# A fused four-layer kernel on one core: the newer attention's first and last units are issued in other places, and its loads in other pieces

## What is computed

```python
x = x + _L0_attn_ref(_layernorm(x))          # older attention
x = x + _L0_ffn_ref(_layernorm(x), ...)      # routed low-rank experts
x = x + _L1_attn_ref(_layernorm(x), ...)     # newer attention
x = x + _L1_ffn_ref(_layernorm(x), ...)      # low-rank experts again

# _L1_attn_ref, cut:
q = _rmsnorm(x @ wq_a.T, q_a_ln_w) @ wq_b.T          # 32 heads of 128
q_nope, q_pe = (q[..., :64], q[..., 64:])
ckv, k_pe = (ckv_kpe[..., :64], ckv_kpe[..., 64:])   # ckv_kpe = x @ wkv_a.T
scores = einsum('bqhd,bkhd->bhqk', q_full, k_full) * softmax_scale   # q_pe and k_pe rotated
attn = softmax(where(causal, scores, min))
out = einsum('bhqk,bkhd->bqhd', attn, v).reshape(B, S, H * 128)
return out @ wo.T
```

## Time and profile before

| | us |
|---|---|
| median of 3 runs (lowest, highest) | 1612.07 (1609.93, 1612.68) |
| the profiled execution: its time, its span | 1615.58, 1613.8 |
| PE busy in the span | 1545.7 (96%) |
| DVE, ACT, POOL busy | 1008.0, 878.5, 811.8 |
| mean granted clock of TensorE | 0.993 |

### The profile page before, as it was taken

One profiled execution on the slowest core, in us unless ns is written; L12 is line 12 of the kernel. 1 busy time (PEld: TensorE's weight loads), 2 busy tenths in 40 slices (PEclk: granted clock), 3 DMA queues, 4 the chain that ended last, 5 costly groups with the idle time before them and its releaser, 6 DMA issues. The chain is left out here.

```text
span 1613.8 us, 31992 instructions
## 1 busy us (share of the span) xinstructions
PE 1545.7 (96%) x12384; PEld 951.8 (59%) x12384; DVE 1008.0 (62%) x2745; ACT 878.5 (54%) x1665; POOL 811.8 (50%) x706
## 2 busy tenths in 40 slices
PE   5998999999989999999999999899999999999998
PEld 4656555555556777777767777644444444466564
DVE  8898767776778888888888888732110100344433
ACT  7787323323759999999999999931210000211110
POOL 4223345446938888888888888720110000244450
PEclk9999999999999999999999999999999999999999
DMA  9993244545829999999999999997763331233331
GB/s 365 306 333 142 67 102 136 154 131 140 156 70 160 192 181 176 191 181 189 187 179 182 192 174 173 181 224 217 176 165 77 96 84 21 82 66 79 92 79 65
DMA packets 556103, 248.78 MB, mean 154 GB/s; under 512 B 498096, under 2 KB 530992, under 8 KB 555824
## 3 DMA queue, kind: packets, MB, share of 16 engines
q1 hardware_dynamic: 555952, 246.74, 66.4%
HBM read 73.68 MB, written 48.23 MB: 76 GB/s over the span
## 5 line engine op out<-in xcount | busy, mean ns | idle before, releaser
L2078 POOL TENSOR_TENSOR xb<-xb 128x1280 f16<-128x1280 f32 x128 | 335.8, 2623 | 8.2 <-ACT xb L1981 8.1
L1973 ACT ACTIVATE xb<-bk,D_sv,qw_c 128x512 f32<-128x512 f32 (+3 forms) x512 | 289.3, 623 | 4.7 <-DVE D_sv L2036 4.4
L2027 DVE TENSOR_REDUCE bk<-bk 128x1 f32<-128x512 f32 (+3 forms) x512 | 227.5, 490 | 18.1 <-PE bk L1923 17.3
L1981 ACT ACTIVATE xb<-xb 128x1280 f16<-128x1280 f32 x128 | 162.6, 1271 | 15.4 <-DMA xb<-xb 11.7
L92 POOL TENSOR_SCALAR mv<-mv 128x1 f32<-128x1 f32 x64 | 28.2, 440 | 280.1 <-DVE mv L87 279.0
L1914 PE MATMUL bk<-kTh,D_QTh 128*128 128x512 f16 (+3 forms) x512 | 153.7, 300 | 6.4 <-ACT xb L1973 6.3
L1915 PE MATMUL bk<-kTl,D_QTh 128*128 128x512 f16 (+3 forms) x512 | 153.4, 300 | 0.0
L1916 PE MATMUL bk<-kTh,D_QTl 128*128 128x512 f16 (+3 forms) x512 | 146.8, 300 | 0.0
L1938 PE MATMUL D_t<-vh,xb 128*128 128x65 f16 x1280 | 132.2, 194 | 5.6 <-DVE D_on L2046 3.5
L1939 PE MATMUL D_t<-vl,xb 128*128 128x65 f16 x1280 | 132.3, 193 | 0.0
L1940 PE MATMUL D_t<-vh,xb 128*128 128x65 f16 x1280 | 131.7, 194 | 0.0
(11 more groups left out here) (355 smaller groups left out, 4385.1 us busy)
## 6 DMA issues: line engine op xcount, KB each, us to landing
od<-D_os SPq DMA_DIRECT2D x32, 512.0 KB, 3.8
xd<-xb SPq DMA_DIRECT2D x16, 512.0 KB, 4.4
ow_raw<-mwd SPq DMA_DIRECT2D x16, 512.0 KB, 4.7
xb<-xd SPq DMA_DIRECT2D x16, 512.0 KB, 5.9
out_x<-xb SPq DMA_DIRECT2D x16, 512.0 KB, 2.8
xb<-in_x SPq DMA_DIRECT2D x6, 1024.0 KB, 13.2
A_wo<-in_wo SPq DMA_DIRECT2D x6, 1024.0 KB, 7.2
ow_raw<-in_w SPq DMA_DIRECT2D x16, 384.0 KB, 4.6
```

What stands on the lines that cost most here:

```text
L1973: m = e.activation(p[:, AT[i]:AT[i] + N], Sb[n % 4][:, c:c + N], ACT.Exp, scale=qw.col(qw.NEG, g), bias=s[:, 7 - i:8 - i])
L1981: e.activation(P2[u % 3][:, 0:1280], P[u % 3][:, :], ACT.Copy).then_inc(s_ph, 1)
L2027: m = e.tensor_reduce(minima(u, i), Sb[n % 4][:, c:c + N], AX.X, ALU.min)
L2078: e.tensor_tensor(P2[u % 3][:, 1280:2560], P[u % 3][:, :], P2[u % 3][:, 0:1280], ALU.subtract).then_inc(s_pl, 1)
```

## The change

It changes the order of the work and the size of some transfers; the same numbers are computed.

- **C, queries and scores.** Queries 0 and 1 are issued behind tile 13 and 2 and 3 behind tile 14, on all engines. Unit 0's turn, its split (`act_high`, `dve_low`) and its scores stand in C's tail, in banks bk0 to bk2. Its split halves lie in `keep`. D starts with unit 1's turn and unit 0's masks.
- **C, weights.** The fourth split of output weights (`ow.act_high(3)`, `ow.dve_low(3)`) moves from D's first units into C's tail. Each raw slice is loaded in two transfers of 256 KB; in C they stand one behind each feed transfer of tiles 4 to 9, and group 0's query weights, one transfer at C's start before, are two behind those of tiles 10 and 11.
- **D, output products.** The slices 0 to 3 of tile j = 2 are multiplied in units 124 to 127, between the first and the second part of the scores, into the query banks. Tiles 0 and 1 get slices 0 to 3 in steps 128 to 131 (129 to 132 before), and slice 4 of all three is in step 132 (`AHEAD` = 5); E starts at slice 5.
- **D, turned pieces.** Pieces p = 0, 1 and 2 of j = 0 to 2 are issued in units 42, 48, 54, 74, 80, 86, 106, 112 and 118. Before, p = 0 was in units 123 to 125, p = 1 in steps 130 to 132, and p = 2 in E.

```diff
 class OutWeights:
-    AHEAD = 4
+    AHEAD = 5
-    def sp_load(self, e, w, kt):
+    def sp_load(self, e, w, kt, halves=(0, 1)):
         w.wait_ge(self.s_ml, kt - 2)
-        e.dma_start(self.raw[kt % 3][:, :].rearrange("p (f n) -> p f n", f=2),
-                    self.mwd[:, :, kt, :].rearrange("f p n -> p f n")).then_inc(self.s_m[kt % 3], 16)
+        for f in halves:
+            e.dma_start(self.raw[kt % 3][:, 512 * f:512 * f + 512], self.mwd[f, :, kt, :]).then_inc(self.s_m[kt % 3], 16)
...
 def projections
   def pe(e):
+        def scores(part):
+            w.wait_ge(s_tl, 4)
+            w.wait_ge(s_vl, (14, 15, 13)[part])
+            qu.pe_scores(e, w, 0, part, bk[part], kT)
...
-            if t >= 2:
+            if 2 <= t < NT - 1:
                 turn_qk(t - 2)
-        query(0)
-        query(1)
+            if t == NT - 3:
+                query(0)
+                query(1)
+            if t == NT - 2:
+                query(2)
+                query(3)
+                turn_qk(NT - 3)
+        w.wait_ge(s_vl, 13)
+        qu.pe_turn(e, w, 0, bk[2], ident)
         turn_qk(NT - 2)
-        query(2)
+        scores(0)
         turn_qk(NT - 1)
-        query(3)
+        scores(1)
+        scores(2)
   def act(e):
...
-        squares(NT - 1)
+            if t >= NT - 2:
+                for u in (2 * (t - NT + 2), 2 * (t - NT + 2) + 1):
+                    qu.act_nope(e, w, u)
+        ow.act_high(e, w, 3)
         high_qk(NT - 3)
         high_v(NT - 2)
-        qu.act_nope(e, w, 0)
-        qu.act_nope(e, w, 1)
+        squares(NT - 1)
+        qu.act_high(e, w, 0, bk[2])
         high_qk(NT - 2)
         high_v(NT - 1)
-        qu.act_nope(e, w, 2)
         high_qk(NT - 1)
-        qu.act_nope(e, w, 3)
   def sp(e):
-        e.dma_start(qu.wb[0][:, :, :, :], wbs[0]).then_inc(s_wb, 16)
         for t in range(3, NT):
             feed.sp_turn(e, w, NT + t)
-            if 8 <= t < 11:
-                ow.sp_load(e, w, t - 8)
+            if 4 <= t < 10:
+                ow.sp_load(e, w, t // 2 - 2, (t % 2,))
+            if 10 <= t < 12:
+                e.dma_start(qu.wb[0][:, t - 10, :, :], wbs[0, :, t - 10, :, :]).then_inc(s_wb, 16)
...
 def attention
-    HIGH, LOW = {-2: 3, NU: 4, NU + 1: 5}, {-1: 3, NU + 1: 4, NU + 2: 5}
+    HIGH, LOW = {NU: 4, NU + 1: 5}, {NU + 1: 4, NU + 2: 5}
   def pe(e):
                 w.wait_ge(s_exp, n - 3)
...
+                qu.pe_scores(e, w, u, part, Sb[n % 4], kT)
+                if part == 0 and u >= NU - 4:
+                    w.wait_ge(s_qn, NU)
+                    w.wait_ge(s_qm, NU)
+                    ow.pe_product(e, w, 2, u - NU + 4)
...
-            if NU < u <= NU + ow.AHEAD:
+            if NU <= u < NU + ow.AHEAD:
                 w.wait_ge(s_exp, 3 * NU)
                 w.wait_ge(s_bias, 2 * NU)
-                w.wait_ge(s_qn, NU)
-                w.wait_ge(s_qm, NU)
-                for j in range(ow.G):
-                    ow.pe_product(e, w, j, u - NU - 1)
+                for j in range(2 if u < NU + 4 else ow.G):
+                    ow.pe_product(e, w, j, u - NU)
   def sp(e):
-            if u == NU - 5:
-                w.wait_ge(s_ot[0], 16 * 15)
-            if NU - 5 <= u < NU - 5 + ow.G:
-                ow.sp_turn_piece(e, u - NU + 5, 0)
-            if NU + 2 <= u < NU + 2 + ow.G:
-                ow.sp_turn_piece(e, u - NU - 2, 1)
+            for p in range(3):
+                for j in range(ow.G):
+                    if u == 42 + 32 * p + 6 * j:
+                        w.wait_ge(s_ot[0], 16 * (4 * p + 3))
+                        ow.sp_turn_piece(e, j, p)
...
 def out_projection
   def sp(e):
-        for p in range(2, 4):
-            if p == 3:
-                w.wait_ge(ow.s_o[0], 16 * G)
-            for j in range(G):
-                ow.sp_turn_piece(e, j, p)
-                ow.sp_load(e, w, next(loads))
+        w.wait_ge(ow.s_o[0], 16 * G)
+        for j in range(G):
+            ow.sp_turn_piece(e, j, 3)
+            ow.sp_load(e, w, next(loads))
```

More of the change, by code:

```diff
@@ L523, in __init__, with pe_turn, act_high, dve_low @@
         self.t2b = [keep[:, 2048 + 256 * i:2304 + 256 * i].rearrange("p (h d) -> p h d", h=4) for i in range(2)]
+        self.QT = [[keep[:, 2560 + 256 * i:2816 + 256 * i].bitcast(H16) for i in range(2)]]
         self.s_q, self.s_qn, self.s_qm, self.s_qr = sem("q"), sem("qn"), sem("qm"), sem("qr")
+        self.s_t, self.s_th, self.s_tl = sem("t"), sem("th"), sem("tl")
     def place(self, sb):
         self.qs += [sb(f"qs{i}", [128, 4, 4, 128]) for i in range(1, 3)]
+        self.QT += [[sb(f"QT{x}", [128, 512], H16) for x in "hl"]]
+    def pe_turn(self, e, w, u, ps, ident):
+        g, b, h = self.UNITS[u]
+        q = self.qs[u // 4 % 3]
+        w.wait_ge(self.s_qn, 4 * (u // 4) + 4)
+        w.wait_ge(self.s_qr, 4 * (u // 4) + 4)
+        w.wait_ge(self.s_tl, u)
+        for tt in range(4):
+            i = e.matmul(ps[:, 128 * tt:128 * tt + 128], q[:, tt, h, :], ident, start=True, stop=True, is_transpose=True)
+        i.then_inc(self.s_t, 1)
+    def act_high(self, e, w, u, ps):
+        w.wait_ge(self.s_t, u + 1)
+        e.activation(self.QT[u % 2][0][:, :], ps[:, :], ACT.Copy).then_inc(self.s_th, 1)
+    def dve_low(self, e, w, u, ps):
+        hi, lo = self.QT[u % 2]
+        w.wait_ge(self.s_th, u + 1)
+        e.tensor_tensor(lo[:, :], ps[:, :], hi[:, :], ALU.subtract).then_inc(self.s_tl, 1)
+    TILES = [(3,), (2,), (1, 0)]
+    def pe_scores(self, e, w, u, part, bank, kT):
+        hi, lo = self.QT[u % 2]
+        k0 = 512 * self.UNITS[u][1]
+        w.wait_ge(self.s_tl, u + 1)
+        c = 0
+        for i in self.TILES[part]:
+            M = 128 * (i + 1)
+            ps = bank[:, c:c + M]
+            qh, ql = hi[:, 128 * i:128 * i + 128], lo[:, 128 * i:128 * i + 128]
+            e.matmul(ps, qh, kT[0][:, k0:k0 + M], start=i > 0, stop=False)
+            e.matmul(ps, qh, kT[1][:, k0:k0 + M], start=False, stop=False)
+            e.matmul(ps, ql, kT[0][:, k0:k0 + M], start=False, stop=False)
+            c += M
     def pe_query(self, e, w, u, s_wb):
@@ L1839, in attention @@
     qu.place(ph.sb)
-    qs, s_q, s_qn, s_qm, s_qr = qu.qs, qu.s_q, qu.s_qn, qu.s_qm, qu.s_qr
-    QT = [(ph.sb(f"QTh{i}", [128, 512], H16), ph.sb(f"QTl{i}", [128, 512], H16)) for i in range(2)]
+    s_q, s_qn, s_qm = qu.s_q, qu.s_qn, qu.s_qm
+    s_t, s_th, s_tl = qu.s_t, qu.s_th, qu.s_tl
     sv = [ph.sb(f"sv{i}", [128, 16]) for i in range(4)]
@@ L1890, in turn_q @@
         def turn_q(u):
[L1891 to L1898, removed]
+            qu.pe_turn(e, w, u, t_bank("t", u), ident)
         def scores(u):
[L1902 to L1905, removed]
             for part in range(3):
@@ L1943, in pe @@
         for u in range(FIRST, LAST):
-            if there(u):
+            if u > 0 and there(u):
                 scores(u)
+                masks(u)
             if there(u - LAG):
                 values(u - LAG)
-            if u < 0:
-                turn_q(u + 2)
+            if u == -1:
+                turn_q(1)
+                masks(0)
             for x in queries(u):
@@ L1987, in high_q @@
         def high_q(u):
[L1988 removed]
             w.wait_ge(s_S, 3 * (u - 1))
[L1990 removed]
+            qu.act_high(e, w, u, t_bank("t", u))
         def high_o(u):
@@ L2011, in act @@
                 ow.act_high(e, w, HIGH[u])
-            for x in queries(u):
+            for x in queries(u) if u >= 0 else []:
                 nope(x)
@@ L2059, in dve @@
                 bias(u, 0)
-            for x in rotations(u):
+            for x in rotations(u) if u else [4]:
                 qu.dve_rotate(e, w, x, cst)
@@ L2067, in dve @@
                 bias(u, 1)
-            if there(u + 2):
+            if u == 0:
+                qu.dve_rotate(e, w, 5, cst)
+            if there(u + 2) and u > -2:
                 low_q(u + 2)
```

50 lines of the change are left out of this document (20 added, 30 removed).

## The result

| | before | after |
|---|---|---|
| median (lowest to highest), us | 1611.24 (1609.76 to 1614.12) | 1599.96 (1599.49 to 1603.75) |
| ratio to before, 95% interval | | 0.9931 (0.992 to 0.9941) |
| the profiled execution, its span | 1615.58, 1613.8 | 1600.77, 1599.0 |

Six runs of each on the same chip. The change is faster by 11.1 us (9.5 to 12.9), 0.7%. I forecast 1603.7, 8.4 less than before, in a range of 1597.5 to 1610.5: sign and range hold, the size is short by a quarter.

What follows compares the result with a forecast made beforehand. PE (96% busy) and ACT were nearly full in D's middle, so gains lay at the seams. Terms -2.0 + 2.5 - 9.9 + 1.0 gave -8.4 us, from the median 1612.07 to 1603.7, range 1597.5 to 1610.5.

Steps and rivals of the forecast that it cites:

- Seam C to D: From C's end into D: unit 0's scores done early bring ACT's exponentials forward; 2.0 us won, ends 0 and 4.
- the feed: PE's wait for its feed in C, 1.08 us at 434.19: a 256 KB load there may give about 0.4 us.
- rival b: Clock falls at C's end and in the drain, costing 4.7 us instead of 1.0: 1607.4; chance 0.16.
- D's middle: Units 42 to 118: nine added pieces delay ACT through transfers; 2.5 us lost, ends 0 and 12.
- nothing for the other seven: In D's middle only the pieces at units 42 and 74 cost an issue; the remaining seven cost 0.
- Tail: D's last units and drain: PE's idle time, waits and slow clock go, less new idle of 1.9; 9.9 us won.
- The 2.09 and 3.46 us: PE's drain gaps, for a transposing transfer and a normalization, both traced to transfers; forecast to go.
- rival d: The drain finds a new wait for normalization, with the clock; half of 9.9 is lost: 1608.7; chance 0.14.
- my 1049.3: At D's end: the time in us near which ACT's last exponentials were forecast to end.
- Clock: Gaps remaining at C's end and in the drain slow PE's clock; 1.0 us charged.
- Rival (a): Pieces stall D's middle each time, 3.19 us each, 28.7 instead of 2.5: 1629.9, slower; chance 0.08.
- (c): Only the tail wins: C ends 3 us later instead of 1.2, the 2.0 is lost: 1605.7; chance 0.14.

Runs made afterwards that it cites:

- again: The kernel before, run unchanged two more times: 1611.34 and 1610.42 us.
- doubled pieces: The changed kernel with each of the nine pieces transferred a second time three units later: 1605.66 us, 0.9961.
- packed pieces: The changed kernel with the nine pieces in neighbouring units 112 to 120: 1607.42 us, 0.9982.
- pieces alone: The kernel before with only the pieces p = 0 to 2 moved to units 42 to 118, products as before: 1607.98 us, 0.9987.
- without the early products: The changed kernel with the j = 2 products moved from units 124 to 127 into steps 128 to 132: 1606.58 us, 0.9969.
- all but the tail: The changed kernel with late pieces, three products a step from 129 and slice 4 in E, as before: 1607.87 us, 0.9987.
- tail alone: The kernel before with only the change's pieces, output products and E's loads; C and the loads as before: 1603.09 us, 0.9955.
- loads alone: The kernel before with only the loads' edit, 256 KB halves at their new places in C: 1609.37 us, 0.9994.

## Why the prediction was right, and where its sizes were off

**Seam C to D, forecast 2.0, measured 3.6 (3.2 against the mean of three executions of before).** The mechanism held: unit 0's scores are ready when D begins, and no query follows the last projection. Unit 1's exponentials, from which on the order is the old one, start 87.6 us after C's start, where before it was 91.3 (477.83): 3.7 earlier. The runs divide that. From D's first turn to unit 1's exponentials it is 12.69 us in all four profiles where the clock fell (465.14 to 477.83 before) and 11.71 and 11.72 in the two where it stayed full, so the slow clock is 1.0. The second "again", whose turn is at 464.97:

```profile
476.69 1.32 ACT L1973 ACTIVATE xb<-bk,D_sv,qw_c 128x512 f32<-128x512 f32 x2
```

PE's waits for the feed in C are 4.3 us before and 3.3 after, so the loads are 1.0, as in the mean of all profiles. What is left, 1.6 to 1.8 by either landmark, is the work moved to C's tail. I had forecast 1.6 for it, and counted from C's start D's first turn and first exponential came 1.5 and 1.6 us sooner than I had them. Query 6's rotation stands behind the first bias as I said, and PE does wait for it, 0.74 us at 467.84. The term that was mis-sized is the feed: I took 0.4, looking at one wait of several. And the clock that before lost at this seam I had only as a price to pay again (rival b, at 1.7 us), not as a gain.

**D's middle, forecast 2.5, measured 1.3 to 1.8 against the other executions, 1.1 between the means.** The size was too large, the places were half right. I put the cost at units 42 and 74, behind weights and a store, and the profiles side by side show it there: ACT waits 0.9 us more beside unit 42 in the mean, and 1.3 more beside unit 74. The pair hides this, since before had dear draws at both. But the three new waits, 2.5 us together, came where a store alone stood ahead. The step that failed is "nothing for the other seven": three of them cost ACT something too. With all nine away from weights and stores the middle shows no cost. ACT's waits are not the time, either: with the pieces ACT waits 3.3 us more in the mean up to unit 121, and the middle is 1.1 us longer. The 0.95 of the transfer engines spoke against a cheap piece. The doubled pieces cost 0.2 to 0.5 us each: the busy share did not say that another transfer would be paid in full. The Trainium skill's 261 GB/s for a transposing transfer with a non-contiguous middle dimension (DMA: Bandwidth & Descriptors, Latency and other measured facts) gives an estimate of 1.0 us for a piece. In time only the packed pieces come near it, at 0.7 us each by the profile.

**Tail, forecast 9.9, measured 10.2 in the pair and 7.8 to 8.3 against the other executions.** The 2.09 and 3.46 us went as forecast, the products filled PE, and no new wait stands in the drain (rival d falls). The last exponentials end 21.6 us after unit 123's mask, where my 1049.3 meant 22.7. With the pieces early and no products among the scores it is 20.7 (pieces alone, and the run without the early products), so the products do delay ACT, by 0.9 us, about what leaving out the stall gives back: the two "again" have 21.5 and 21.4. That both waits go back to transfers held in part: with the pieces alone 3.15 us of normalization waits stay, where the two waits were 5.55. Two things more were missed. The split loads cost 0.8 us at E's start: I had counted one issue more on SP as covered, but behind the last store nothing covers it, since all engines meet there. And the baseline's drain varies by 2 us from execution to execution with where one transfer's wait falls, so a gain read from one profile is uncertain by as much.

The tail's parts help one another, which one execution could not tell me: pieces alone give 1.4 to 1.8 us in the drain and lose 1.6 to 2.1 in the middle in their one profile; the early products add 4.2, of which 3.3 is PE's four waits for exponentials. The products were not run without the early pieces: with p = 0 issued in units 123 to 125, product 0 of unit 124 would wait for a transfer that has just begun.

**Clock, forecast 1.0 lost, measured 0.** It stayed at 1.00 at both seams, although PE has a turn, three small gaps and the block's end at the first (rival b falls). The Trainium skill (TensorE: Matmul & The Clock Gate, Part 4: PE-mode transpose) has transposes not count as work for the clock, which spoke for rival (b): in all eight profiles with unit 0's turn in C's tail the stretch behind D's start has 1.00. So these transposes and gaps did not bring the fall that the rule would favour.

That the sum is only a quarter short is in part luck. Against the other executions the tail's gain was forecast 1.6 to 2.1 us too large and the seam's 1.2 too small, the middle's loss 0.7 to 1.2 too large, and the clock's 1.0 did not come; the first error hides a part of the others.

Rival (a) falls by the doubled pieces, (c) by the run of all but the tail, which wins at the first seam by itself. The packed pieces show what (a) described: it is real, but needs neighbouring units.

## What to carry to other kernels

Work for the next stage that PE can do in a seam is worth its length, and here the clock's 1.0 us besides: with it the clock stayed full in eight profiles of eight, without it in two of six. Look for it in both directions. A small transfer beside a full queue is cheap where no other extra issue stands near, so place it halfway between the others and not by an even stride, and keep issues away from a block's end, where no engine covers them. Before forecasting a few us in a drain from one profile, take a second execution of the same kernel, and compare a single wait only with the same wait in several: what the split costs, and what the pieces of units 42 and 74 cost, shows only so.

## What the runs showed of the hardware that was not expected

- The clock fell in some executions and not in others. With the same instructions of PE around D's start and a gap of 2.70 to 2.75 us, the 6 us behind D's start had 0.72 in before, the first "again", the pieces alone and the tail alone, and 1.00 in the second "again" and the loads alone. From D's first turn to its first mask this is 5.5 us or 4.2. Where the gap is 0.73 it did not fall in eight profiles. What decides it is not shown. The two executions of before, from the busy time by stretch:

```profile
464.10:470.10 6.00, 6.00 (x32) 3.66 (x33) 3.51 (x7) 2.62 (x4) 1.03 (x3) 0.72 0.27 87
```

```profile
464.90:470.90 6.00, 5.81 (x38) 3.45 (x39) 4.29 (x8) 2.51 (x4) 1.15 (x3) 1.00 0.26 87
```

- The same instruction on DVE takes 2.40 us in the drain and 1.28 one step later. POOL is at work on a unit's low part in the first case; that this is the cause was not tried. Timeline of DVE after:

```profile
1046.26 2.40 DVE L659 SCALAR_TENSOR_TENSOR ow_ml<-ow_raw,ms_c,ow_mh 128x1024 f16<-128x1024 f32 x1 [1.60 <-ACT ow_mh L655]
...
1049.64 1.28 DVE L659 SCALAR_TENSOR_TENSOR ow_ml<-ow_raw,ms_c,ow_mh 128x1024 f16<-128x1024 f32 x1
```

- After, a 256 KB transposing transfer among D's units is issued on SP in 1.30 to 1.42 us when it stands alone, and in 1.52 to 2.77 right behind a store. A direct load of 256 KB takes 0.56 us (2.24 for four) behind D's last store and 0.40 to 0.53 (0.80 to 1.06 for two) a few us later.
